# A two-layer gated cross-attention and mixture-of-experts kernel: the first layer's gate and up matmuls from high and low halves, and three smaller edits

## The reference

```python
x = x + jnp.tanh(g_xattn[0]) * _L0_xattn_ref(_layernorm(x), ctx_1024, ctx_1024, mask, ...)
x = x + jnp.tanh(g_ffn[0]) * _L0_ffn_ref(_layernorm(x), ...)
x = x + jnp.tanh(g_xattn[1]) * _L1_xattn_ref(_layernorm(x), ctx_1024, ...)
x = x + jnp.tanh(g_ffn[1]) * _L1_ffn_ref(_layernorm(x), ...)
```

```python
w, idx = jax.lax.top_k(softmax(x @ gate_w), 8);  w = w / sum(w)
gu_e = jnp.einsum('ech,ehf->ecf', buf, expert_gate_up_w)     # 512 -> 2 x 256
act = silu(gu_e[..., :256]) * gu_e[..., 256:]
out_e = jnp.einsum('eci,eih->ech', act, expert_down_w)       # 256 -> 512
y = sum over the 8 experts of out_e[e, slot] * w
```

## Time and profile before

| | |
|---|---|
| median of 3 runs | 2229.95 us (2222.38 to 2230.94) |
| the profiled execution | 2234.43 us, of which its span is 2232.7 |
| TensorE's granted clock, mean | 0.976 |
| TensorE busy (modelled ends) | 2101.4 us, 94% |
| VectorE / ScalarE / GpSimd busy | 1309.2 / 1050.2 / 525.9 us |
| data moved | 288.22 MB, mean 129 GB/s |
| first gate-and-up matmul of the layer 0 experts | 697.3 us |
| last one | 1118.0 us |

### The profile page before, as it was taken

The page is one execution under the profiler, slowest core; times in us unless marked ns, Lnnn a source line. Parts: engine busy times, 40 slices in busy tenths (PEclk is TensorE's granted clock), DMA queues, the critical chain, the costliest instruction groups (busy, mean ns, idle before and its releaser), DMA issues. The chain is left out here.

```text
span 2232.7 us, 39855 instructions
## 1 busy us (share of the span) xinstructions
PE 2101.4 (94%) x13454; PEld 1518.1 (68%) x13455; DVE 1309.2 (59%) x2799; ACT 1050.2 (47%) x2427; POOL 525.9 (24%) x503
## 2 busy tenths in 40 slices
PE   6999999997998999999978999999979989999998
PEld 4777777785964444444456777777858867777775
DVE  4577777776773222222255777777663437777776
ACT  2466666666321111111134666666654316666655
POOL 3000000001553555454511000000013302223331
PEclk9999999997999999999999999999979999999999
DMA  5011001103142999999831000000031156656661
GB/s 183 31 33 34 18 22 33 33 23 115 39 188 83 340 305 326 328 336 291 269 96 54 28 28 14 17 28 28 28 113 72 39 201 237 255 202 226 226 222 17
DMA packets 63758, 288.22 MB, mean 129 GB/s; under 512 B 10626, under 2 KB 10796, under 8 KB 44292
## 3 DMA queue, kind: packets, MB, share of 16 engines
q1 hardware_dynamic: 43892, 247.41, 30.0%
q0 software_dynamic: 19728, 38.97, 8.0%
HBM read 259.82 MB, written 32.93 MB: 131 GB/s over the span
## 5 line engine op out<-in xcount | busy, mean ns | idle before, releaser
L796 ACT ACTIVATE probs<-ps,less_max 100x360 f32<-100x360 f32 (+1 forms) x384 | 212.3, 562 | 168.3 <-DVE less_max L626 88.8
L1786 PE MATMUL pgu<-ring,xT 128*128 x560 | 267.1, 600 | 8.1 <-issue 3.5
L782 ACT ACTIVATE pTs<-pt 128x300 f32<-128x300 f32 x512 | 190.0, 426 | 125.4 <-PE pt L505 124.2
L1786 PEld LDWEIGHTS pgu<-ring,xT 128*128 128x128 f32 x560 | 99.4, 191 | 116.9 <-issue 116.4
L505 PE MATMUL pt<-ident,probs 100*128 100x100 f32 (+1 forms) x1152 | 139.0, 259 | 29.5 <-ACT pTs L782 26.2
L505 PEld LDWEIGHTS pt<-ident,probs 100*128 100x128 f32 (+1 forms) x1152 | 117.5, 142 | 60.3 <-issue 36.7
L1874 DVE COPY hT<-ph 128x256 f32<-128x256 f32 x70 | 29.7, 425 | 197.3 <-PE ph L1792 197.3
L382 PE MATMUL po<-first 128*128 128x512 f32 (+1 forms) x564 | 143.6, 404 | 1.4 <-DVEq L684 1.4
L382 PE MATMUL pp<-first 128*128 128x512 f32 x564 | 143.0, 402 | 1.2 <-DVE first L406 1.2
L626 DVE CUSTOM_DVE_ANT_0 ps<-ps,madd 100x362 f32<-100x362 f32 (+1 forms) x256 | 128.8, 565 | 23.9 <-PE ps L491 23.6
L378 PE MATMUL po<-first 128*128 128x362 f32 (+1 forms) x720 | 138.5, 342 | 2.8 <-DVE first L415 1.4
(11 more groups left out here) (352 smaller groups left out, 4457.0 us busy)
## 6 DMA issues: line engine op xcount, KB each, us to landing
ring<-in_l_ew SPq DMA_DIRECT2D x64, 1536.0 KB, 9.1
w<-in_l_ew SPq DMA_DIRECT2D x40, 1024.0 KB, 7.6
after<-in_l_ew SPq DMA_DIRECT2D x24, 1024.0 KB, 8.1
xnT<-in_ctxT SPq DMA_DIRECT2D x14, 1444.0 KB, 6.6
first<-in_l_up SPq DMA_DIRECT2D x2, 4096.0 KB, 13.4
b<-in_l_eb SPq DMA_DIRECT2D x8, 1024.0 KB, 4.7
wd<-in_l_down SPq DMA_DIRECT2D x2, 2048.0 KB, 8.1
xn_rows<-mid SPq DMA_DIRECT2D x16, 200.0 KB
```

Source lines behind the costliest of these rows:

```text
L782: act.activation(pTs[:, g % 2, j, 3 * half:3 * half + 3, :].rearrange("k c q -> k (c q)"), pt[:, half, 0:3 * S], ACT.Copy).then_inc(t_out, 1)
L796: act.activation(probs[g % 2 * HPC + j][:, k0:k1], ps[j][0:S, 0:k1 - k0], ACT.Exp, bias=less_max[:, g, seg, j:j + 1], scale=-1.0 if masked ...
L1786: last = pe.matmul(pgu[p][:, :], xT[p][:, c, :], wgu[c], start=c == 0, stop=c == DC - 1)
```

## The change

Four edits. In the layer 0 experts gate and up are made from high and low halves: `xT` holds the next tile's rows as high and low, `ws[p]` the gate-and-up weights of a tile in halves. ScalarE makes the high parts (`x_high_out`, and `split_high` two tiles ahead), VectorE the low ones (`rows_out`, and `split_low` one tile ahead); TensorE waits for `gu_low` and `x_ready` and no longer for `w_ready`, and its two value loads there go, while ScalarE gets two per tile and VectorE one. The tables get two more entries, so that the splits may run past the last tile. SyncE waits for `parts_done` before its last two loads. The adding DMA leaves out slots of no row (`bounds_check`), and the zeroing of the two `moe_sum` ends goes.

In both attentions the last batch's two pieces `("k", 3, 0)` and `("k", 3, 1)` are made in its own halves 4 and 5, and not beside the batch before. In the dense part of layer 1 the wait for `x_out` moves behind the gelu of chunk 4, and the high parts of the hidden rows follow 4 chunks later instead of 1.

```diff
@@ attention: the zeroing, and the pieces of the last batch
-                        for sums in env.moe_sums:
-                            sp.dma_start(sums[T:TOKEN_ROWS, :], zrow[:, :]).then_inc(rows_zeroed, 16)
...
-                        sp.wait_ge(rows_zeroed, 3 * 16)
+                        sp.wait_ge(rows_zeroed, 16)
...
+        LATE = {4: (("k", 3, 0),), 5: (("k", 3, 1),)}
+        LATE_ONES = LATE[4] + LATE[5]
+        LAST_PIECES = [x for x in PIECES if x not in LATE_ONES] + list(LATE_ONES)
...
+        def beside(b, h):
+
+            if b == B - 1:
+                return b, LATE.get(h, ())
+            return b + 1, tuple(x for x in BESIDE[h] if b + 1 < B - 1 or x not in LATE_ONES)
@@ dense part of layer 1, ScalarE
+        LAG = 4
...
-                    act.wait_ge(x_out, 16 * B)
-                    act.wait_ge(x_low, 2)
...
-                        if 1 <= n <= NP_ // 2:
-                            high_of_hidden(n - 1)
+                        if n == LAG:
+
+                            act.wait_ge(x_out, 16 * B)
+                            act.wait_ge(x_low, 2)
+                        if LAG <= n < NP_ // 2 + LAG:
+                            high_of_hidden(n - LAG)
@@ routing tables
+                        link(dve.tensor_copy(env.tile_expert[:, NT:NT + 2], texp[:, NT - 1:NT].broadcast_to([1, 2])))
...
+                        link(dve.tensor_copy(env.tile_buffer[:, NT:NT + 2], texp[:, NT - 1:NT].broadcast_to([1, 2])))
@@ experts_swiglu
-        xT = [sb(f"xT{p}", [P, DC, P]) for p in range(2)]
+        xT = [sb(f"xT{part}", [P, DC, P], F32R) for part in ("_high", "_low")]
...
+        ws = [[sb(f"ws{p}{part}", [P, DC, 2 * I0], F32R) for part in ("_high", "_low")] for p in range(2)]
...
+        def gate_up_weights(engine, t):
+            at = slice(t, t + 1) if isinstance(t, int) else bass.ds(t, 1)
+            place = engine.value_load(env.tile_buffer[0:1, at], min_val=0, max_val=RING - 1)
+            return ring[:, bass.ds(place, 1), 0:DC, :].rearrange("p a c n -> p (a c) n")
@@ SyncE
+                sp.wait_ge(parts_done, 1)
                 sp.dma_start(env.bk_ahead[:, :], env.kv_ahead[2]).then_inc(rest_in, 16)
@@ GpSimd, add_rows
-                        out_offset=bass.IndirectOffsetOnAxis(ap=sum_at[p][:, 0:1], axis=0)).then_inc(added[p], 16)
+                        out_offset=bass.IndirectOffsetOnAxis(ap=sum_at[p][:, 0:1], axis=0),
+                        bounds_check=T - 1, oob_is_err=False).then_inc(added[p], 16)
@@ TensorE
                 def gate_up(t, p, between):
-                    at = slice(t, t + 1) if isinstance(t, int) else bass.ds(t, 1)
-                    e = pe.value_load(env.tile_expert[0:1, at], min_val=0, max_val=E0 - 1)
-                    wgu = weights(t, 0)
-                    pe.wait_ge(w_ready, e + 1)
+                    pe.wait_ge(gu_low, t + 1)
                     pe.wait_ge(x_ready, t + 1)
...
-                        last = pe.matmul(pgu[p][:, :], xT[p][:, c, :], wgu[c], start=c == 0, stop=c == DC - 1)
+                        for i, j in PARTS:
+                            last = pe.matmul(pgu[p][:, :], xT[i][:, c, :], ws[p][j][:, c, :],
+                                             start=c == 0 and (i, j) == PARTS[0],
+                                             stop=c == DC - 1 and (i, j) == PARTS[-1])
@@ ScalarE
+                def x_high_out(t):
+                    act.wait_ge(x_mm, t + 1)
+                    act.activation(xT[0][:, :, :], px[:, :, :], ACT.Copy).then_inc(x_high, 1)
+
+                def split_high(t, p):
+                    at = slice(t, t + 1) if isinstance(t, int) else bass.ds(t, 1)
+                    e = act.value_load(env.tile_expert[0:1, at], min_val=0, max_val=E0 - 1)
+                    wgu = gate_up_weights(act, t)
+                    act.wait_ge(w_ready, e + 1)
+                    act.activation(ws[p][0][:, :, :], wgu, ACT.Copy).then_inc(gu_high, 1)
+
+                def units(t, p):
+
+                    silu(t, p)
+                    x_high_out(t + 1)
+                    split_high(t + 2, p)
...
                 with act.Fori(2, n_pairs) as i:
-                    silu(i * 2, 0)
+                    units(i * 2, 0)
                     row_out(i * 2 - 1, i - 1, 1)
-                    silu(i * 2 + 1, 1)
+                    units(i * 2 + 1, 1)
                     row_out(i * 2, i, 0)
...
+                act.wait_ge(gu_low, last_pair * 2 + 3)
+                act.sem_inc(parts_done, 1)
@@ VectorE
-                def rows_out(t, p):
-                    dve.wait_ge(x_mm, t + 1)
-                    dve.tensor_copy(xT[p][:, :, :], px[:, :, :]).then_inc(x_ready, 1)
+                def rows_out(t):
+                    dve.wait_ge(x_high, t + 1)
+                    dve.tensor_tensor(xT[1][:, :, :], px[:, :, :], xT[0][:, :, :].bitcast(F32), ALU.subtract)\
+                        .then_inc(x_ready, 1)
+
+                def split_low(t, p):
+                    wgu = gate_up_weights(dve, t)
+                    dve.wait_ge(gu_high, t + 1)
+                    dve.tensor_tensor(ws[p][1][:, :, :], wgu, ws[p][0][:, :, :].bitcast(F32), ALU.subtract)\
+                        .then_inc(gu_low, 1)
...
                     if not first:
                         hidden_out(t - 1, 1 - p)
-                    rows_out(t + 1, 1 - p)
+                    split_low(t + 1, 1 - p)
+                    rows_out(t + 1)
                     hidden(t, p)
```

More of the change, by code:

```diff
@@ L344, in bank_of_heads, with pieces_in_order, number, piece_before @@
             return (pp, po)[g % 2]
-        def piece_before(what):
-            before = [x for x in PIECES[:PIECES.index(what)] if bank_of(x) is bank_of(what)]
-            return PIECES.index(before[-1]) + 1 if before else 0
-        def bank_free(pe, what, b):
-            if what == ("k", 0, 0):
+        def pieces_in_order(b):
+            return LAST_PIECES if b == B - 1 else PIECES
+        def number(what, b):
+            return b * NPIECE + pieces_in_order(b).index(what) + 1
+        def beside(b, h):
+            if b == B - 1:
+                return b, LATE.get(h, ())
+            return b + 1, tuple(x for x in BESIDE[h] if b + 1 < B - 1 or x not in LATE_ONES)
+        def piece_before(what, b):
+            order = pieces_in_order(b)
+            before = [x for x in order[:order.index(what)] if bank_of(x) is bank_of(what)]
+            return order.index(before[-1]) + 1 if before else 0
+        def bank_free(pe, what, b):
+            if b == B - 1:
+                if what == ("k", 3, 0):
+                    pe.wait_ge(piece_out, b * NPIECE + NPIECE - len(LATE_ONES))
+                else:
+                    pe.wait_ge(ao_ready, b * NG + 1)
+            elif b == B - 2 and what == ("v", 3):
+                pe.wait_ge(ao_ready, b * NG + 3)
+            elif what == ("k", 0, 0):
                 pe.wait_ge(piece_out, b * NPIECE + NPIECE)
@@ L363, in bank_free @@
             else:
-                pe.wait_ge(piece_out, b * NPIECE + (NPIECE + piece_before(what)))
+                pe.wait_ge(piece_out, b * NPIECE + (NPIECE + piece_before(what, b + 1)))
         def make_piece(pe, what, b, first_batch=False):
             pk = bank_of(what)
-            if first_batch and piece_before(what):
-                pe.wait_ge(piece_out, piece_before(what))
+            if first_batch and piece_before(what, 0):
+                pe.wait_ge(piece_out, piece_before(what, 0))
             end = SEG[what[2]][1] if what[0] == "k" else what[1] * P + keys_of(what[1])
@@ L389, in piece_high @@
                 m, (k0, k1) = what[1], SEG[what[2]]
-                act.wait_ge(piece_mm, b * NPIECE + PIECES.index(what) + 1)
+                act.wait_ge(piece_mm, number(what, b))
                 act.activation(kT[0][:, m, k0:k1], bank_of(what)[:, 0:k1 - k0], ACT.Identity,
@@ L404, in piece_rest @@
                 kc = what[1]
-                dve.wait_ge(piece_mm, b * NPIECE + PIECES.index(what) + 1)
+                dve.wait_ge(piece_mm, number(what, b))
                 dve.tensor_copy(v[p][0:keys_of(kc), kc, :], pk[0:keys_of(kc), :]).then_inc(piece_out, 1)
@@ L531, in outputs @@
                     if more:
-                        pe.wait_ge(piece_out, b * NPIECE + (NPIECE + PIECES.index(("v", 4)) + 1))
+                        pe.wait_ge(piece_out, number(("v", 4), b + 1))
                     for c in range(DC):
@@ L580, in piece @@
                         bank_free(pe, what, b)
-                        make_piece(pe, what, b + 1)
+                        make_piece(pe, what, beside(b, 4)[0])
                     for h in HALVES:
@@ L586, in body @@
                         turn = h < NHALF + 2 or left
-                        pieces = BESIDE[h] if left else ()
+                        _, pieces = beside(b, h)
                         if h % 2 == 0:
@@ L593, in body @@
                             transposed(tb, tg, 2 * late)
-                        if pieces:
```

(23 more changed lines are left out.)

26 lines of the change are left out of this document (16 added, 10 removed).

## The result

The changed kernel takes 2301.3 us (median of 4 runs, 2296.8 to 2307.8) against 2228.2 before: the ratio is 1.0336, 95% interval 1.0317 to 1.0355, so it is 3.4% or 73 us slower. I had forecast 2228 and a range up to 2262. The profiled execution of the changed kernel has a span of 2295.1 us, 62.4 more than the one of before.

The account below looks back on a forecast made before the run. TensorE is busy nearly throughout the experts; after the change VectorE's loop bounds them. Terms +0.7 + 5.3 + 1.2 - 6.0 - 3.3 = -2.1 gave 2232.3, the runs' median 4.5 lower: 2228 us, range 2196 to 2262.

Parts of the forecast that it names:

- it just fits, once per tile: Experts: GpSimd's scatter, index, gather and second copy take 3.7 us; the next VectorE subtraction begins 3.75 after release.
- I add 0.05 per tile: Experts: allowance for what shows of the gathers' time, making 6.05 us per tile, +0.7 us in all.
- Rival (b): Experts: GpSimd falls behind, gathers come late, TensorE waits; 2252 us at 6.4 per tile, 2272 at 6.7; chance 0.25.
- The loop: Experts: VectorE's path per tile, 1.9 + 0.9 (value load) + 2.22 + 0.69 + 0.29 = 6.00 us.
- rival (a): Experts: VectorE's value load is hidden under the hidden copy, loop 5.52 us, 2196 us in all; chance 0.22.
- ScalarE: Experts: ScalarE's high part starts at S + 6.0, S being gate-and-up's start; it keeps up with 0.6 us to spare: 0.
- Rival (c): Experts: the DMA engines are the bound already, so the stage stays at 6.04 per tile, 2227 us; chance 0.08.
- Start: Start of the experts' stage: value loads, high and low part come before the first matmul, +5.3 us.
- End: End of the experts' stage: high and low parts made for tiles that don't exist, +1.2 us.
- my 0 for the loads: End of the experts' stage: SyncE's last two loads, now later, cost 0, at most +3 us.
- Attention: Both attentions: two key pieces moved into the last batch's own halves gain 3.0 us per layer, -6.0 in all.
- Dense part: Second layer's dense part: the wait for the store of x moves behind the fifth result, -3.3 us.

Follow-up runs that it names:

- run 2: Changed kernel, but ScalarE instead of GpSimd makes the two index copies of each tile: 2242.7 us.
- run 3: Changed kernel, but VectorE's weight subtraction is replaced from the third tile on by four instructions with one PSUM operand, writing zeros: 2244.8 us.
- run 5: Changed kernel with a useless 0.42 us VectorE copy from PSUM per tile, between the low parts of weights and rows: 2253.7 us.
- run 4: Changed kernel, but VectorE loads the register with the weights' place before waiting for the transposed hidden rows: 2285.1 us.
- run 6: Changed kernel, but ScalarE makes a tile's scaled output ahead of the weights' high part: 2256.6 us.
- run 7: Changed kernel with index copies on ScalarE, early value load, scaled output first, and the weights' low part in two halves around the rows: 2229.6 us.
- run 9: Kernel of run 7, but from the seventh expert on the down weights are not loaded: 2203.1 us.
- run 11: Kernel before with only the moved attention key pieces: 2225.7 us, ratio 0.9994.
- run 12: Kernel before with only the later wait and the lag in layer 1's dense part: 2222.2 us, ratio 0.9985.

## Why the prediction was wrong

**The step that failed** is "it just fits, once per tile", and with it "I add 0.05 per tile". My 3.7 us was right as the time from a release to the start of the second copy (3.61 measured); but I had called it scatter, index, gather and second copy, and by my own prices these five numbers (1.59, 0.18, 0.85, 1.08, 0.20) are 3.90; only up to the copy's start, which is what decides, are they 3.70. I compared it with 3.75, a tile of 6.04 less 2.29; with my loop's own 6.00 it would have been 3.71. VectorE's loop came out at 5.86 in a tile that waits for nothing, so the room is 3.57. A margin of 0.01 to 0.05 us inside a sum of five terms was no margin. The second stretch shown above, 3.73, is another part of the chain: gap, scatter, index copy, gap, up to the gather's start. And a miss is not paid in hundredths: an instruction that starts 0.04 late is held for nearly all of the 2.29. Runs 2, 3 and 5 each give the room back in another way (less for GpSimd, no exclusion, a longer tile), and each brings back 47 to 59 us.

**Rival (b)** was this mechanism, with its place and the point from which it decides. Its price was too low: I spread one more held instruction over several tiles (6.4 to 6.7), but GpSimd then lacks 1.1 us in tile after tile until the pause comes, and behind the pause the granted clock is 0.66: 6.96.

**The loop**, term by term, from the starts of a tile that waits for nothing (831.92, then 833.81, 834.74, 836.95, 837.78): 1.89 to the hidden copy (1.9), 0.93 to the low part (0.9), 2.21 to the rows (2.22), 0.83 to TensorE (0.98). The sum is 5.86 against 6.00. The value load, of which I had been least sure, was right: the wait of the copy in front holds it (the copy starts at 833.81, the load at 833.91). With this **rival (a)** is out, and run 4 shows that the 0.5 can be had by a move in the order. The Trainium skill, TensorE: Matmul & The Clock Gate, section Architectural detail, gives VectorE a strict queue of 8. Had the copy's wait stood in that queue, the load would have run ahead; the 0.93 shows that it did not.

**ScalarE** starts the high part at S + 6.1 in a tile that waits for nothing and the low part waits for it little in the changed kernel (18.8 us in 68 tiles): right, and run 6 shows how thin it is.

**Rival (c)**, the DMA engines, is not what made this kernel slower (its DMA share is 0.83), but it keeps the mended version of run 7 at 5.96 (run 9). I gave it 0.08 and should have seen that it limits the gain of rival (a) too: at full bytes no run came below 5.89 per tile.

**Start** +5.3: 4.7 to the first matmul, which is what I had added up (5.7 - 1.0), 5.5 to the second tile (13.1 - 7.6). **End** +1.2, at most 3 more: 5.4 measured (54.3 us from the last gate-and-up to layer 1's queries against 48.9). Of this 2.2 is TensorE's wait at the end of the stage. It is this row:

```profile
1201.72 9.74 PE L69 MATMUL pk<-first 128*128 128x362 f32 x48 [3.89 <-PEq L2419]
```

TensorE sat idle for 3.89 there, 1.72 before. It isn't the postponed loads: these land at 1194.6, and then SyncE itself waits 5.4 us for the others (SyncE's waits from 1150 on; us in total, times, longest):

```profile
SPq L1696 <- DMA first<-in_l_wq: 7.0, 1, 7.0
SPq L1696 <- PEq L1696: 5.4, 1, 5.4
```

GpSimd is last: its last scatter starts at 1188.30 and has landed by 1195.9, and GpSimd ends the block with a drain from 1196.07 to 1199.98, 2.1 us after TensorE's (1197.85). In the kernel before it ended at 1134.71, 0.8 ahead of TensorE's 1135.52. So my 0 for the loads was right, and the late GpSimd, which I hadn't priced there, costs here too. **Attention** -6.0: -1.3 by run 11, at most -4.0, and what there is of it in layer 0. **Dense part** -3.3: -3.3 by run 12. I had these four terms at -2.8 together; measured they are some +6, off by 9 us; the one on GpSimd was off by 62.

## What to carry to other kernels

Where one engine's instructions hold another's for as long as they last, ask how much of the held one's chain must fit between two of them; if the margin is below the error of the sum, missing it needs a large share of the chance. A miss can cost nearly a whole instruction per round, and the lag grows until the buffers are used up. Moving small copies off the engine that is held (58.6 us here), or even lengthening the other engine's round (47.6), can be worth more than a saving on TensorE; and before saving there at all, see whether the DMA share leaves anything to gain.

## What I had not expected of the hardware

- The exclusion goes by the start. A gather that starts 0.16 us ahead of the subtraction takes its 1.08 us beside it (run 5); one that starts 0.07 behind takes 3.17. An index copy directly behind a scatter is held even where its record begins 0.3 to 0.4 ahead (846.22 against 846.55), since that record begins inside the scatter's.
- Only GpSimd pays. In the changed kernel all 68 subtractions of the stage take 2.29 us, also the one with a gather started 0.03 us and the one with a scatter started 0.13 us ahead of it.
- It holds for the gather and scatter instructions as for copies: 1.07 becomes up to 3.19 us, the second copy's 0.2 up to 2.3.
- The stage's first tile is made at a low clock in both kernels. In the changed one TensorE sat idle for 5.75 us before it, the granted clock between 696 and 701 is 0.50, and matmuls of 128x512 take 0.63 us instead of 0.40; before, behind idle times of 2.48 and 1.03, it was 0.66 between 697 and 702. The twelve faster matmuls take 5.3 us there and the eight slower ones 5.1, so the first tile gives back nothing of what the split saves.
